# Single batches' expert down products in three fp16 passes, rests on GpSimd, rotary products ahead of the norm

## The reference

```python
x = x + _L0_attn_ref(_layernorm(x), ...)   # 16 heads of 8, 4 key groups, l2-normed q and k, rotary, causal
x = x + _L0_xattn_ref(_layernorm(x), ctx_512, ctx_512, ...)
x = x + _L0_ffn_ref(_layernorm(x), ...)    # 8 experts by token place, gelu
x = x + _L1_attn_ref(_layernorm(x), ...)   # mLSTM recurrence
x = x + _L1_xattn_ref(_layernorm(x), ctx_512, ...)   # causal self attention plus cross attention
x = x + _L1_ffn_ref(_layernorm(x), ...)
```

```python
q = q / (sqrt(sum(q * q)) + 1e-10)
q = concatenate([x1 * cos - x2 * sin, x2 * cos + x1 * sin])
```

```python
h = relu(einsum('td,ehd->teh', xf, w1) + b1)          # 128 -> 512
expert_out = einsum('teh,edh->ted', h, w2) + b2       # 512 -> 128
out = einsum('ted,te->td', expert_out, combine)
```

## Time and profile before

| | before |
|---|---|
| three timed runs, median (lowest to highest) | 365.16 us (364.35 to 366.58) |
| profiled execution | 363.92 us |
| its span in the trace | 362.1 us |
| mean granted clock of PE, of full | 0.948 |
| instructions | 8932 |
| PE / DVE / ACT / POOL busy | 312.8 / 281.5 / 212.0 / 88.3 us |

### The profile page before, as it was taken

One profiled execution on the slowest core, in us unless ns is written; L12 is line 12 of the kernel. 1 busy time (PEld: TensorE's weight loads), 2 busy tenths in 40 slices (PEclk: granted clock), 3 DMA queues, 4 the chain that ended last, 5 costly groups with the idle time before them and its releaser, 6 DMA issues.

```text
span 362.1 us, 8932 instructions
## 1 busy us (share of the span) xinstructions
PE 312.8 (86%) x3256; PEld 215.8 (60%) x3256; DVE 281.5 (78%) x746; ACT 212.0 (59%) x377; POOL 88.3 (24%) x196
## 2 busy tenths in 40 slices
PE   0747999886997885976899999999999999999994
PEld 0533345554596664744545657887766697767773
DVE  6876757999767767999997899998813477889894
ACT  1348786664664773645566957335466645865660
POOL 2773688444242403600001220001100004000000
PEclk9995699999899996698899999999999999999999
DMA  6940000000000046000000000000000000000001
GB/s 177 415 188 1 2 3 2 3 2 2 2 1 4 0 176 289 1 2 2 0 2 3 3 2 2 1 2 2 2 16 0 5 0 2 0 16 3 2 2 29
DMA packets 4187, 12.33 MB, mean 34 GB/s; under 512 B 490, under 2 KB 2802, under 8 KB 3122
## 3 DMA queue, kind: packets, MB, share of 16 engines
q1 hardware_dynamic: 4146, 11.77, 8.9%
HBM read 11.24 MB, written 0.52 MB: 33 GB/s over the span
## 4 chain that ended last, share of the span: by engine, by line
PE 43%; DVE 11%; issue 2%; ACT 2%; POOL 1%; DVEq 0%; ACTq 0%; POOLq 0%
PE double L1813 10%; PE single L1837 6%; PE single L1826 5%; PE single L1487 3%; PE single L1479 3%; DVE mx L1305 3%; PE double L1700 2%; PE double L1535 2%; PE outs L1584 2%; PE double L1531 2%; DVE mxc L1292 2%; PE double L1696 2%; PE outs L1592 1%; PE outs L1572 1%; PE double L1837 1%
## 5 line engine op out<-in xcount | busy, mean ns | idle before, releaser
L935 ACT ACTIVATE region_p<-double 128x1024 f32<-128x1024 f32 x64 | 64.4, 1024 | 24.9 <-PE double L1535 10.8
L759 POOL TENSOR_SCALAR rstd<-mv 128x2 f32<-128x2 f32 x24 | 5.9, 246 | 169.9 <-DVE mv L1117 169.2
L1813 PE MATMUL double<-xnT,w 128*128 128x256 f16 (+1 forms) x252 | 39.7, 308 | 0.0
L1305 DVE TENSOR_REDUCE mx<-double 128x4 f32<-128x1024 f32 (+1 forms) x24 | 29.4, 1226 | 1.8 <-PE double L1700 0.9
L1813 PEld LDWEIGHTS double<-xnT,w 128*128 128x128 f16 x252 | 23.8, 98 | 11.5 <-issue 0.8
L1045 ACT ACTIVATE hidden<-double,b1s 128x256 f32<-128x256 f32 x48 | 18.7, 478 | 18.6 <-PE double L1813 18.6
L1837 PE MATMUL single<-w,hidden 128*128 128x128 f32 x224 | 27.8, 278 | 0.2 <-DVE hidden L1184 0.2
L1459 DVE SCALAR_TENSOR_TENSOR x<-single,comb,x 128x128 f32<-128x128 f32 x60 | 17.5, 344 | 12.0 <-PE single L1837 9.7
L1837 PEld LDWEIGHTS single<-w,hidden 128*128 128x128 f32 x224 | 26.1, 192 | 1.2 <-issue 0.4
L1826 PEld LDWEIGHTS single<-w,hidden 128*128 128x128 f16 x384 | 22.0, 98 | 3.2 <-DVE hidden L1441 1.5
L1826 PE MATMUL single<-w,hidden 128*128 128x128 f16 x384 | 22.8, 219 | 1.3 <-DVE hidden L1441 1.3
(11 more groups left out here) (281 smaller groups left out, 714.2 us busy)
## 6 DMA issues: line engine op xcount, KB each, us to landing
w<-in_w1a SPq DMA_DIRECT2D x2, 1024.0 KB, 11.2
w<-in_w2a SPq DMA_DIRECT2D x2, 1024.0 KB, 13.2
w<-in_w1b SPq DMA_DIRECT2D x2, 1024.0 KB, 7.8
w<-in_w2b SPq DMA_DIRECT2D x2, 1024.0 KB, 10.6
row<-in_row SPq DMA_DIRECT2D x1, 800.0 KB, 7.6
wb<-in_wb SPq DMA_DIRECT2D x1, 709.0 KB, 8.7
x<-in_x SPq DMA_DIRECT2D x4, 128.0 KB, 3.1
out<-x SPq DMA_DIRECT2D x4, 128.0 KB, 1.8
```

The source lines that it names most:

```text
L935: a.activation(probs[:, slot("prob", key), :], psum(step), ACT.Exp, scale=SCALE).then_inc(psum_done[PSUM.slot(step)], 1)
L1305: gives(step, v.tensor_reduce(dst, psum(step).rearrange("p (r g k) -> p r g k", r=2, k=k), X, ALU.max))
L1813: ins = mm(o if w == T else two(o), w1s[e][:, w_part, c * P:(c + 1) * P], xs[:, b, x_part] if w > T else xs[:, b % 2, x_part, b // 2, :], ...
```

## The change

The single batches' `mdown` takes the same three fp16 passes as the pair's, 24 products of 128x128x128 in place of 8 in fp32. So every group has an `hs`: the fp16 part on ACT, and the rest on DVE for the pair and on POOL for single batches. The relu of a single batch goes to the two slots of `hid0` and no longer straight to `hidden`. The rests of w1 and w2 go from DVE to POOL, in two instructions each: w is multiplied by 64 in place, then the fp16 part is subtracted. `w2s` no longer waits for single batches' `mdown`, only for the first layer's last use of the place in `wb` where its first result lies, so it can stand much earlier. In the head `ropea` is cut: squares and sums stay, the root is a step of its own, `roper`, and the rotary products are formed from the undivided q and k in a new step `ropec` ahead of the division. The order table and the list for DVE are new throughout.

```diff
-        add(("ropea", b), [("qkv", b)], ("A", 0.32), ("D", 0.49), ("A", 0.4))
-        add(("ropeb", b), [("ropea", b), ("presets0", 0)], ("D", 4.1), ("G", 3.0))
-        hold("rope", b, ("ropea", b), ("ropeb", b))
+        add(("ropea", b), [("qkv", b)], ("A", 0.47), ("D", 0.49))
+        add(("roper", b), [("ropea", b)], ("A", 0.3))
+        add(("ropec", b), [("ropea", b), ("presets0", 0)], ("D", 2.1))
+        add(("ropeb", b), [("ropec", b), ("roper", b)], ("D", 2.1), ("G", 3.0))
+        hold("rope", b, ("ropea", b), ("ropea", b))
...
+            for q in range(n):
+                add(("hs", g, e, q), [("mup", g, e, q)], ("A", 1.06),
+                    ("D", 1.23) if n == 2 else ("G", 2.9), behind=[q and ("hs", g, e, 0)])
+                hold("hid0", (g, e, q), ("mup", g, e, q), ("hs", g, e, q))
...
-    1, 12, 20, 13, 0, 14, 15, 28, 4, 29, 3, 2, 21, 30, 5, 16, 36, 31, 38, 17, 32, 22, 6, 33, 7, 8,
...
+    1, 2, 14, 34, 24, 15, 16, 4, 17, 35, 25, 0, 5, 18, 36, 19, 3, 20, 21, 6, 44, 37, 26, 38, 7, 8,
...
-        w2s = [(w1[:, NE - 1, :] if e == 0 else w2[:, e - 1, :, :].rearrange("p c n -> p (c n)"))
+        w2s = [(wb[:, 0:4 * P] if e == 0 else w2[:, e - 1, :, :].rearrange("p c n -> p (c n)"))
-        out_scale = lambda b: WSCALE ** 2 if b in GROUPS[HALVED] else WSCALE
+        out_scale = WSCALE ** 2
...
+                elif kind == "ws":
+
+                    e = step[1]
+                    pool.wait_ge(sem("w_high"), e + 1)
+                    then(g.tensor_scalar(w1[:, e, :], w1[:, e, :], WSCALE, None, ALU.mult))
+                    then(g.tensor_tensor(w1s[e][:, 1, :], w1[:, e, :], w1s[e][:, 0, :], ALU.subtract),
+                         "w_split")
+                elif kind == "w2s":
+
+                    e = step[1]
+                    flat = lambda ap: ap.rearrange("p c n -> p (c n)")
+                    pool.wait_ge(sem("w2_high"), e + 1)
+                    then(g.tensor_scalar(flat(w2[:, e]), flat(w2[:, e]), WSCALE, None, ALU.mult))
+                    then(g.tensor_tensor(flat(w2s[e][:, 1]), flat(w2[:, e]), flat(w2s[e][:, 0]),
+                                         ALU.subtract), "w2_split")
+                elif kind == "hs" and len(GROUPS[step[1]]) == 1:
+
+                    pool.wait_ge(sem("hidden_high"), count(("hs",), step))
+                    then(g.tensor_tensor(half_of(step, 1), relus(step), half_of(step, 0), ALU.subtract),
+                         "single_low")
...
                     if last is not None:
-                        act.wait_ge(sem("rope_done"), count(("ropeb",), last))
+                        act.wait_ge(sem("sums_ready"), count(("ropea",), last))
                     then(a.activation(sq[:, slot("rope", b)], raw[:, b], ACT.Square), "squares_ready")
-                    act.wait_ge(sem("sums_ready"), count(("ropea",), step))
+                elif kind == "roper":
+                    act.wait_ge(sem("sums_ready"), count(("ropea",), ("ropea", b)))
                     then(a.activation(nrm[:, b, :], nrm[:, b, :], ACT.Sqrt), "norms_ready")
...
-                    act.wait_ge(sem("w_split"), NE + e)
-                    for g in range(len(GROUPS)):
-                        if e and g != HALVED:
-                            act.wait_ge(psum_full, PSUM.full(("mdown", g, e - 1)))
+                    if e == 0:
+                        for n in range(NB):
+                            act.wait_ge(psum_full, PSUM.full(("nxa", n)))
+                    else:
+                        act.wait_ge(sem("w2_split"), e)
...
+                elif kind == "ropec":
+
+                    dve.wait_ge(sem("rope_tables"), 4)
+                    s = raw[:, b]
+                    then(v.tensor_tensor(swp[:, :, 0:4], s[:, :, 4:8], sinx[:, :, 0:4], ALU.mult), wait=False)
+                    then(v.tensor_tensor(swp[:, :, 4:8], s[:, :, 0:4], sinx[:, :, 4:8], ALU.mult))
+                    then(v.tensor_tensor(s, s, cosx, ALU.mult))
+                    then(v.tensor_tensor(s, s, swp, ALU.add), "rope_turned")
-                    dve.wait_ge(sem("norms_ready"), count(("ropea",), ("ropea", b)))
-                    dve.wait_ge(sem("rope_tables"), 4)
-                    s = sq[:, slot("rope", b)]
+                    dve.wait_ge(sem("norms_ready"), count(("roper",), ("roper", b)))
                     then(v.tensor_scalar(nrm[:, b, :], nrm[:, b, :], 1e-10, None, ALU.add))
                     then(v.reciprocal(nrm[:, b, :], nrm[:, b, :]))
-                    then(v.tensor_tensor(s, raw[:, b], nrm[:, b, :].unsqueeze(2).to_broadcast([P, 40, HD]),
-                                         ALU.mult))
...
-
-                    then(v.tensor_tensor(rot, s, cosx, ALU.mult), wait=False)
-                    then(v.tensor_tensor(swp[:, :, 0:4], s[:, :, 4:8], sinx[:, :, 0:4], ALU.mult), wait=False)
-                    then(v.tensor_tensor(swp[:, :, 4:8], s[:, :, 0:4], sinx[:, :, 4:8], ALU.mult))
-                    then(v.tensor_tensor(rot, rot, swp, ALU.add), "rope_done")
+                    then(v.tensor_tensor(rot, raw[:, b], nrm[:, b, :].unsqueeze(2).to_broadcast([P, 40, HD]),
+                                         ALU.mult), "rope_done")
...
+                    low_ready(pe, ("hs", g, e, len(GROUPS[g]) - 1))
+                    pe.wait_ge(sem("w2_split"), e + 1)
+                    dst, hid = take(step), halves[slot("hidden", (g, e))]
                     for i in range(2 * len(GROUPS[g])):
                         for c in range(HC):
-                            ins = mm(dst[:, i * P:(i + 1) * P], hid[:, c, i * P:(i + 1) * P],
-                                     w2[:, e, c, :], start=c == 0, stop=c == HC - 1)
+                            for m, (h_part, w_part) in enumerate(((0, 0), (0, 1), (1, 0))):
+                                ins = mm(dst[:, i * P:(i + 1) * P], hid[:, h_part, c, i * P:(i + 1) * P],
+                                         w2s[e][:, w_part, c, :], start=c == m == 0,
+                                         stop=c == HC - 1 and m == 2)
```

More of the change, by code:

```diff
@@ L662, in read_by_tensor, with relus, half_of, low_ready @@
                 eng.wait_ge(psum_full, PSUM.full(step))
+        def relus(step):
+            return hid0[:, slot("hid0", step[1:])].rearrange("p (c n) -> p c n", c=4 // len(GROUPS[step[1]]))
+        def half_of(step, n):
+            _, g, e, q = step
+            w, m = T * len(GROUPS[g]), 4 // len(GROUPS[g])
+            return halves[slot("hidden", (g, e))][:, n, m * q:m * q + m, 0:w]
+        def low_ready(eng, step):
+            kinds = [s for s in ORDER[:INDEX[step] + 1] if s[0] == "hs"
+                     and len(GROUPS[s[1]]) == len(GROUPS[step[1]])]
+            eng.wait_ge(sem("hidden_low" if len(GROUPS[step[1]]) == 2 else "single_low"), len(kinds))
         def relus_free(eng, step):
@@ L670, in relus_free @@
                 eng.wait_ge(sem("hidden_high"), count(("hs",), last))
-                eng.wait_ge(sem("hidden_low"), count(("hs",), last))
+                low_ready(eng, last)
         def slot(pool, holder):
@@ L1044, in _ @@
                         c = n * q + k
[L1045 removed]
+                        a.activation(dst[:, k, :], psum(step)[:, k * w:(k + 1) * w], ACT.Relu,
                                      bias=b1s[:, e * HC + c:e * HC + c + 1]).then_inc(
```

94 lines of the change are left out of this document (21 added, 73 removed), and 55 rows, old and new, of the table ORDER_TABLE.

## The result

The changed kernel takes 378.13 us (median of 4 runs, 376.04 to 381.75), the kernel before 364.75 on the same chip (363.33 to 366.58). The ratio is 1.034 with a 95% interval of 1.029 to 1.040: it is slower by 3.4%, where 356.5 us was forecast. The profiled execution took 377.87 us, its span 376.1, the mean granted clock was 0.918 (0.948 before).

The account below looks back on a forecast made before the run. PE, DVE and a latency chain were taken to rule in turn, with POOL having room. 363.9 - 7.2 - 3.5 - 1.4 + 1.5 + 2.0 = 355.3, plus 1.2 for timed runs: 356.5 us, range 351 to 366.

Parts of the forecast that it names:

- Clock: Rival, 140 to 180 us: PE, fed by a freer DVE, keeps 2.4 GHz longer, about 5 us less; 351 us, chance 0.04.
- DVE and POOL together, +2: From 180 to 318 us, DVE's SBUF-only operations stretch beside busy POOL; most finds room; +2 us, between 0 and 24.
- the 24 given as the worst: Upper bound, 180 to 318 us, for the stretching of DVE's SBUF-only operations beside POOL's new work: 24 us.
- a sign of being wrong: After 180 us: the prediction is wrong if DVE becomes the engine that PE waits for.
- the port rival: Small DVE operations, 165 to 308 us, beside POOL's splits and rests: 16 us on the path, 370.5 us, chance 0.12.
- Passes, -7.2: Single experts' 16 down products, fp32 to fp16: 1.34 us each in place of 1.79, -7.2 us in all.
- Rests, covered: Single experts: POOL's rests, 2.34 us each, leave POOL not full, and ACT's waits for them are covered by PE's work.
- junction, +1.5: Before the pair's first up product: POOL's rests delay batch 2's norm and x split, +1.5 us, between 0 and 4.7.
- The ring of relu, copy and rest: Single experts: two relu buffers turn once in 5.0 us for two experts, while PE spends at least 5.5.
- Head, -3.5: Start of the kernel: POOL's constants first and rotary products ahead of the norm bring earlier first scores, -3.5 us.
- Splits off DVE, -1.4: Only the two of 16 weight splits starting before 180 us, in DVE's own stage, count: -1.4 us, between 0 and -11.0.

Follow-up runs that it names:

- e16: Kernel before with the new rotary part and the new order up to its 333rd step, without its second-weight steps; fp32 down products, splits on DVE: 376.1 us, ratio 1.031.
- e10: Changed kernel with 18 filler products on PE between 172 and 186 us and all splits of weights back on DVE: 371.44 us.
- e11: e6 with single experts' rests on POOL cut from 1024 columns to 2 and lower halves filled with zeros near 150 us: 363.87 us, ratio 0.996.
- e6: Changed kernel with 18 filler products that nobody reads, on PE between 172 and 186 us: 372.33 us, ratio 1.013.

## Why the prediction was wrong

**The order, put at nothing.** This is the main step that failed: the sum priced what each edit adds or removes, and took the rest of the table for neutral, with the earlier trace rows of the old order as the frame. By the kernels above: head -6.8, new order of the steps behind it +19.5, all else of the change up to lna.4.2 -2.4, the single experts +3.7, together +14.0, as the last column of the table of events has it. Of e16's 19.5 us, 17.8 are busy time of PE between lna.2.0 and lna.4.2, with 58.0 us at the lower level in place of 13.7. Which of the moved steps leave PE short of work there was not taken apart.

**Clock.** It was weighed as a gain only (351 us, chance 0.04). It was a loss, 5.8 us by the fillers in the changed kernel, and by the busy times the form that most of the order's cost took. The stage in question, 140 to 180 us, already had a mean of 0.77 with PE idle a quarter of it; that less work there could lower the clock further was not priced.

**DVE and POOL together, +2.** This step failed too, in size. The text said that most of the stretching finds room. The chain's DVE instructions lasted 9.6 us longer than their shortest behind lna.4.2, against 0.8 before: 8.8 us on the path. Over the whole trace the excess by line and shape rose from 10.1 to 27.4 us, 17.3 of the 24 given as the worst. For the splits it came out even: with them on DVE (e10) 8.4 us of the excess go, 11.0 us of splits come back, and the time hardly moves. For the rests it did not: that DVE becomes the engine that PE waits for after 180 us was named as a sign of being wrong, and it came. So the port rival had this mechanism right, at about half of its 16 us on the path; that its sum, 370.5 us, was the nearest to 378.1 is luck, since it lacks the order.

**Passes, -7.2.** Right: 1.35 us measured for 1.34, and PE's busy time from lna.4.2 to the last update fell by 5.5 us after and by 8.0 in e11. The gain was covered by 9.1 us more of idle time after.

**Rests, covered; junction, +1.5.** The ring of relu, copy and rest held: neither ACT nor PE waited for a rest. From batch 2's last projection (314.48) to the pair's first up product (324.87) it was 10.4 us in place of 9.4, +1.0.

**Head, -3.5.** The place was right: POOL's key cast came at 16.55 and the first scores at 22.78. The size was 6.8 us, and it was not two effects that add: rotary part and order are worth nothing or less alone.

**Splits off DVE, -1.4.** At most 1 to 2 us, and of the other sign (e10 against e6). POOL's scaling took 1.5 us, not the select's 0.66; it didn't matter.

## What to carry to other kernels

A new order of the same work is an edit like any other: price it first, by running the old arithmetic in it. Work that is moved to an idle engine can cost by what it does to its neighbour: look at which small instructions of the other engine run beside it, and whether they lie on the path; that nobody waits for the moved work proves nothing. An engine of higher speed can be the worse place for it if it has to stand and wait. Compare the bound engine's busy time for the same instructions in both kernels: where it rises, look at the clock before the waits. Where that clock is at its lower level in some stage, ask of each change what it leaves that engine to do just ahead of it; a few products that nobody reads can be worth 6 us.

## What was not expected of the hardware

POOL's in-place scaling of 512 fp32 elements takes 1.5 us, more than its two-input subtraction of as many (1.2) and than twice its select (0.66). A small DVE operation with two inputs from SBUF can last as long as a POOL rest. In the changed kernel's timeline:

```profile
319.45 2.13 POOL L862 TENSOR_TENSOR hidden<-hid,hidden 128x1024 f16<-128x1024 f32 x1 [0.78 <-ACT hidden L1038]
319.62 0.17 DVE L1433 RECIPROCAL gex<-gex 128x2 f32<-128x2 f32 x1
...
319.82 1.78 DVE L1434 TENSOR_TENSOR gex<-gex 128x2 f32<-128x2 f32 x1
```

The product of two elements ends at 321.60, when the rest ends (321.58); the reciprocal with one input, beside the same rest, took 0.17. That is the rule of the Trainium skill cited in the prediction (SBUF — State Buffer, "Who interferes with whom"), and the trace agrees. But the two-input ones are not alone: three of the six instructions on the chain (mxc and mx L1340, xn L1154) are TENSOR_SCALAR with one tensor input, and took 0.94, 1.62 and 1.55 us where their shortest take 0.18 and 0.33. Whether a stretched instruction costs anything depends on the chain: those beside the splits cost no more than the splits do on DVE itself (e10), and the six beside the rests lie on the chain with 8.0 us.
